# An end of its own for the program behind the last scores: other order on ScalarE, GpSimd and VectorE, and other PSUM banks

## Chip, cores and metric

The kernel runs on one core of one Trainium2 chip. The metric is the device time of one execution in microseconds (us). Engines are written as in the profile: PE is TensorE, PEld its weight loads, ACT ScalarE, DVE VectorE, POOL GpSimd, SP SyncE (it only issues DMAs). Each engine works through its own list of instructions in order and waits for semaphores.

## What is computed

One transformer layer over 16 batches of 256 rows and 128 columns, in float32. Cut to what matters:

```python
x = x + attention(x)            # 16 heads, window of 128, "genetic fitness" weights, exp, values, Wo
x = layernorm(x)
xq = fp4_round(x)               # blocks of 16: scale = max|x| / 6, rounding to the grid 0 .5 1 1.5 2 3 4 6
h = silu(xq @ fp4_round(w_gate).T) * (xq @ fp4_round(w_up).T)      # 352 columns
x = layernorm(x + fp4_round(h) @ fp4_round(w_down).T)
```

## The kernel before

Every batch x goes through some ten stages, and a loop over `t` from -3 works on several batches at once: the scores, exponentials and values of batch t, the projection and first layernorm of batch t - 1, gate and up of the first half of batch t - 2, the second half of batch t - 3, its rounding, the product with w_down ("down") and the second layernorm of batch t - 4. All five engines carry this loop written out, with the same `t`, and the order in each of them is the order of the source. A batch's 256 rows are two halves k = 0 and 1 of 128 rows each. In the 15 iterations or so in the middle PE, DVE and ACT fill each other's gaps.

The last scores belong to batch 15 (B - 1) and are given out at t = 15. What stands behind is the subject here. At t = 16 batch 15 is projected, and from t = 17 to t = 20 nothing is left but the tail: for batches 13, 14 and 15 these steps, each with the engine that does it.

1. `gate_up(x, k)` on PE writes two banks; half 0 goes to WC and WD, half 1 of the last three batches to S bank 0 and 1. `tanh(x, k)` on ACT (line 639, `th`), `gate` and `up` on DVE (lines 1215 and 1222, `hh` and `h`).
2. `h_scale` on DVE (line 1242 to 1250, ends in `hr`), `h_over_scale` on POOL (lines 501 and 505, `hn`), `step_of_h` on ACT (line 616, `hu`), `round_h` on DVE (line 1234 twice for each half, `hm`), `h_times_scale` on POOL (line 511, `hq`).
3. PE turns hq (line 916), for half 0 into WC and for half 1 into WD, at t > 16 into S bank 2. ACT copies it to `hqT` (line 664), and PE multiplies by w_down (line 933) into WD.
4. `residual_2` (line 1202), `sums_2` (line 1169) and `aggr_2` (line 1182) on DVE, `norm_2` on POOL (lines 517 to 522, four small instructions, `rstd` and `nb`), `apply_2` on ACT (line 602, `yo`), and SP stores `yo`.

For the rows of x that go into `gate_up` there is a shorter way: `apply_1` (ACT, `y1`, also line 602), `quant_x` on DVE in seven steps 0 to 6 (line 1259 `xmax` to line 1265 `xn`, then 1269, 1272 and 1276 `xm`), with `step_of_x` on ACT (line 623, `xu`) between step 3 and step 4, then PE turns `xm` (line 966) and ACT copies it to `xaT` (line 706).

Two rules tie batches together. `norm_2(x)` on POOL begins with `need(pool, s_yo, NT * x)`: it waits until ACT has applied batch x - 1, since both use the same small tiles. And `mv2`, `hm`, `hq` and `hqT` exist once, so that each step waits for the readers of the batch before.

Before, the tail is what the loop makes of t = 16 to 20, with conditions such as `if t == B + 1` for the places at which the order should differ. On ACT these are, at the end of t = 16, `apply_1` of batch 15, `apply_2(11)` and `apply_2(12)`, and at t = 17 `tanh(14, 1)`, `step_of_x(15)`, the copies of h^T of batch 13, and so on. On POOL `norm_2(x - 1)` stands between the two halves of `h_times_scale(x)`.

## Time and profile before

| | us |
|---|---|
| median of 3 runs | 336.33 |
| lowest and highest | 336.30, 337.07 |
| profiled execution, its own time | 335.8 |
| span of its trace | 333.8 |
| mean granted TensorE clock, as a share of 2.4 GHz | 0.955 |

| engine | busy us | share of the span |
|---|---|---|
| PE | 264.9 | 79% |
| DVE | 253.2 | 76% |
| ACT | 213.0 | 64% |
| POOL | 198.6 | 59% |

The span is the trace from its first to its last event; 2.0 us of the execution's time lie around it. The busy shares are means over the whole program. In the page's line of 40 slices the digits of PE are 8 and 9 up to slice 35 and then 6, 3, 5, 5, 4, 1: the last 42 us or so are another regime than the middle, and the change lies in them.

### The profile page before, as it was taken

Reading aid. Unit: us, or ns where it says so; the run is one execution under the profiler, and the core shown is the slowest. Engines: PE = TensorE matmul, PEld = TensorE weight load, DVE = VectorE, ACT = ScalarE, POOL = GpSimd, SP = SyncE. Lnnn points to the kernel's source line nnn. Section 1 sums busy time; section 2 is a strip of 40 time slices with the busy share of each in tenths; the row PEclk is TensorE's granted clock in tenths of the full one; section 3 lists DMA queues with packets and bytes.
Section 4 is the critical chain, followed back from the end, with each engine's and each line's share of the span. In section 5 each row is a group of like instructions: output and inputs, shape, how many; then the busy total and the mean of one; then the engine's idle time right before and its main releaser. Section 6 shows DMA issues by size and latency. Waiting matters only on the chain. (4 is left out here: it accounts for less than half of the span.)

```text
span 333.8 us, 12978 instructions
## 1 busy us (share of the span) xinstructions
PE 264.9 (79%) x5044; PEld 177.6 (53%) x5044; DVE 253.2 (76%) x697; ACT 213.0 (64%) x515; POOL 198.6 (59%) x471
## 2 busy tenths in 40 slices
PE   5515778989798998989898989998989999635541
PEld 3313344655466665757575666666656665514330
DVE  5723369476989898989898899999888897836631
ACT  2101535586869787877878787978788896433231
POOL 6363545346485778686869686777873553442541
PEclk9999999999999999999999999999999999975855
DMA  4032112122123313340522233223312100010000
GB/s 120 16 63 50 32 33 49 36 49 51 33 50 35 60 24 84 29 86 20 81 34 65 45 57 40 61 66 34 51 33 60 26 20 18 0 32 2 16 16 21
DMA packets 42884, 14.19 MB, mean 43 GB/s; under 512 B 35586, under 2 KB 42820, under 8 KB 42820
## 3 DMA queue, kind: packets, MB, share of 16 engines
q1 hardware_dynamic: 42820, 13.33, 20.8%
q8 instruction: 41, 0.67, 0.8%
q14 instruction: 23, 0.19, 0.2%
HBM read 2.84 MB, written 2.10 MB: 15 GB/s over the span
## 5 line engine op out<-in xcount | busy, mean ns | idle before, releaser
L596 ACT ACTIVATE Pm<-S 128x384 f32<-128x384 f32 x256 | 112.2, 495 | 51.4 <-PE S L788 51.2
L809 PE MATMUL OT<-Pm,gv 128*32 128x256 f32 (+1 forms) x1024 | 58.3, 348 | 0.0
L782 PE MATMUL S<-BT,AT 32*32 32x160 f16 (+4 forms) x2048 | 41.0, 224 | 16.9 <-ACT Pm L596 10.6
L511 POOL TENSOR_TENSOR hq<-hm,hs 128x352 f32<-128x352 f32 x32 | 24.9, 795 | 36.8 <-DVE hm L1234 36.8
L782 PEld LDWEIGHTS S<-BT,AT 32*32 32x32 f16 x2048 | 17.8, 88 | 50.6 <-ACT Pm L596 34.3
L933 PE MATMUL WD<-wdT,hqT 128*128 128x128 f32 (+1 forms) x192 | 29.0, 307 | 14.7 <-ACT hqT L664 14.7
L809 PEld LDWEIGHTS OT<-Pm,gv 128*32 128x32 f32 x1024 | 27.6, 113 | 20.9 <-issue 8.2
L933 PEld LDWEIGHTS WD<-wdT,hqT 128*128 128x128 f32 (+1 forms) x192 | 25.8, 213 | 17.4 <-ACT hqT L664 17.4
L788 PE MATMUL S<-mask,ident 32*32 32x96 f16 x1024 | 31.3, 207 | 0.0
L853 PE MATMUL WA<-wgv,xT 128*128 128x256 f32 x64 | 22.8, 489 | 4.6 <-DMA bgrow<-bg_dram 3.5
L505 POOL TENSOR_TENSOR hn<-h,hrn 128x352 f32<-128x352 f32 x32 | 25.4, 815 | 1.3
L842 PE MATMUL WC<-wguT,xaT 128*128 128x352 f32 x58 | 24.9, 511 | 0.9 <-ACT xaT L696 0.5
L520 POOL TENSOR_TENSOR rstd<-ve,mhalf 128x2 f32<-128x2 f32 x32 | 23.1, 723 | 0.0
L602 ACT ACTIVATE yo<-y,nb,rstd 128x128 f32<-128x128 f32 x32 | 14.0, 491 | 13.0 <-POOL nb L522 13.0
L843 PE MATMUL WD<-wguT,xaT 128*128 128x352 f32 x58 | 21.9, 459 | 0.0
L557 POOL TENSOR_TENSOR A<-gh,A 128x512 f16<-128x512 f32 x16 | 20.4, 1277 | 0.2
L616 ACT ACTIVATE hu<-hn,off 128x352 f32<-128x352 f32 x32 | 17.6, 615 | 3.4 <-POOL hn L505 3.4
L1215 DVE SCALAR_TENSOR_TENSOR hh<-th,WC 128x352 f32<-128x352 f32 x29 | 14.4, 496 | 5.7 <-ACT th L639 5.4
L1234 DVE SCALAR_TENSOR_TENSOR hm<-hu,hn 128x352 f32<-128x352 f32 x32 | 16.9, 527 | 1.8 <-ACT hu L616 1.8
L683 ACT ACTIVATE gsq<-WA 128x256 f32<-128x256 f32 x16 | 6.2, 386 | 18.7 <-PE WA L857 14.2
L1234 DVE SCALAR_TENSOR_TENSOR hm<-hu,hm 128x352 f32<-128x352 f32 x32 | 17.1, 533 | 0.5
L853 PEld LDWEIGHTS WA<-wgv,xT 128*128 128x128 f32 x64 | 13.3, 231 | 7.7 <-POOL ones L445 3.5
(161 smaller groups left out, 633.6 us busy)
## 6 DMA issues: line engine op xcount, KB each, us to landing
xT<-x_turned_dram SPq DMA_DIRECT2D x16, 128.0 KB, 2.3
...
AT<-A SPq DMA_TRANSPOSE x32, 2.5
BT<-B SPq DMA_TRANSPOSE x32, 2.5
...
```

Source lines behind the costliest of these rows:

```text
L505: pool.tensor_tensor(b3(hn[:, k]), b3(h[:, k]), bc(hrn[:, k], QB), ALU.mult).then_inc(s_hn, 1)
L511: pool.tensor_tensor(b3(hq[:, k, 0:I]), b3(hm[:, k]), bc(hs[:, k], QB), ALU.mult).then_inc(s_hq, 1)
L520: pool.tensor_tensor(r[:, :], ve[:, :], mhalf[:, 0:NT], ALU.pow).then_inc(s_out, 1)
L596: act.activation(Pm[:, group % PR, hd % 4, :], S[:, (H * x + hd) % 3, 0:SCW], ACT.Exp, scale=1.0 / ZS).then_inc(s_exp, 1)
L782: pe.matmul(S[k0:k0 + KG, bank, at:at + n], AT[r:r + 32, x % 2, c, q:q + KG], BT[r:r + 32, x % 2, c, q:q + n], start=(kt == 0), stop=False)
L788: i = pe.matmul(S[k0:k0 + KG, bank, 0:SCW].rearrange("p (b c) -> p b c", c=P)[:, :, k0:k0 + KG], ident16[m:m + KG, m:m + KG], near[m:m + K ...
L809: i = pe.matmul(OT[VP * g:VP * (g + 1), T - (q1 - q0):T], gv_flat[:, at:at + VP], Pm[:, (GROUPS * x + c) % PR, g, q0:q1], start=(kt == 0 a ...
L842: pe.matmul(g, lhs, wguT[:, 0:I], start=True, stop=True).then_inc(s_gate, 1)
L843: pe.matmul(u, lhs, wguT[:, I:2 * I], start=True, stop=True).then_inc(s_gu, 1)
L853: pe.matmul(WA[:, k * 2 * D:(k + 1) * 2 * D], xT[:, (t + 3) % XR, k * P:(k + 1) * P], wgv[:, :], start=(k == 0), stop=False)
L933: i = pe.matmul(WD[:, k * D:(k + 1) * D], hqT[0:kn, k, n * P:(n + 1) * P], wdT[0:kn, n, :], start=(n == 0), stop=(n == 2))
L1234: dve.scalar_tensor_tensor(out=hm[:, k], in0=hu[:, k], scalar=ROUND, in1=hm[:, k] if step else hn[:, k], op0=ALU.max, op1=op).then_inc(s_h ...
```

## The change

The loop over `t` now ends at t = 16 (B) on PE, ACT, DVE and POOL, and the tail is written out behind it on each engine. SP keeps its loop. Same instructions, same number (2153 on PE, 863 on DVE by the program order); what differs is their order and some banks:

- ACT: `tanh(14, 1)` goes ahead of `apply_1` of batch 15, and so ahead of `apply_2(11)` and `apply_2(12)`. The copies of h^T of batch 13 go ahead of these two as well, the `step_of_x` of batch 15 stays behind them. `tanh(15, 1)` goes ahead of `apply_2(13)`, and the last copies of h^T ahead of `apply_2(14)`.
- POOL: both halves of `h_times_scale(x)` go ahead of `norm_2(x - 1)`, for batches 13, 14 and 15.
- DVE: `residual_2`, `sums_2` and `aggr_2` of batch 14 come ahead of the four rounding steps of batch 15, no longer between them.
- PE: the order is the same. The turned hq goes to OT (half 0) and WA (half 1), not to WC and S bank 2, and "down" to S bank 2, not to WD. The waits that go with the banks differ: before, the turned hq of half 0 waited for `h(x + 1, 0)`; now "down" of batch x waits for `residual_2(x - 1)`.

```diff
 # POOL
-            for t in range(FIRST, LAST + 1):
+            for t in range(FIRST, B + 1):
...
-                if live(t - 4) and not late(t - 4):
-                    norm_2(t - 4)
                 if live(t - 3):
                     h_times_scale(t - 3, 1)
+            norm_2(B - 4)
+            for x in (B - 2, B - 1):
+                h_over_scale(x, 0)
+                h_over_scale(x, 1)
+                h_times_scale(x, 0)
+                h_times_scale(x, 1)
+                norm_2(x - 1)
+            norm_2(B - 1)
 # ACT
-                if t == B:
-                    apply_1(t + 1)
-                if live(t - 5) and late(t - 5):
+                if live(t - 5) and t < B:
                     apply_2(t - 5)
-                if live(t - 4) and not late(t - 4):
-                    apply_2(t - 4)
+            def hqT_out(x):
+                for k, bank in enumerate((OT, WA)):
+                    act.wait_ge(s_hqT, NT * x + k + 1)
+                    need(act, s_dn, x)
+                    act.activation(hqT[:, k, :], bank[:, 0:HP], ACT.Copy).then_inc(s_hqTc, 1)
+            tanh(B - 2, 1)
+            apply_1(B + 1)
+            hqT_out(B - 3)
+            apply_2(B - 5)
+            apply_2(B - 4)
+            step_of_x(B - 1)
+            step_of_h(B - 2, 0)
+            step_of_h(B - 2, 1)
+            act.wait_ge(s_xqT, B)
+            act.wait_ge(s_gu, NT * (B - 1))
+            act.activation(xaT[:, T:2 * T], WC[:, T:2 * T], ACT.Copy).then_inc(s_xac, 1)
+            tanh(B - 1, 0)
+            tanh(B - 1, 1)
+            hqT_out(B - 2)
+            apply_2(B - 3)
+            step_of_h(B - 1, 0)
+            step_of_h(B - 1, 1)
+            hqT_out(B - 1)
+            apply_2(B - 2)
+            apply_2(B - 1)
 # PE
+            def hqT_last(x):
+                if x == B - 3:
+                    pe.wait_ge(s_ot, 2 * B)
+                    pe.wait_ge(s_attn, B)
+                else:
+                    pe.wait_ge(s_hqTc, NT * x)
+                for k, bank in enumerate((OT, WA)):
+                    pe.wait_ge(s_hq, NT * x + k + 1)
...
+            def down_last(x):
+                if x > B - 3:
+                    pe.wait_ge(s_ln2, 5 * (x - 1) + 1)
+                for k in range(NT):
+                    pe.wait_ge(s_hqTc, NT * x + k + 1)
+                    for n, (k0, kn) in enumerate(KC):
+                        i = pe.matmul(S[:, 2, k * D:(k + 1) * D], hqT[0:kn, k, n * P:(n + 1) * P], wdT[0:kn, n, :],
...
 # DVE
+            gate(B - 2, 1)
+            up(B - 2, 1)
+            for step in range(3):
+                h_scale(B - 2, step)
+            for step in range(7):
+                quant_x(B - 1, step)
+            down_norm(B - 3)
+            rounds(B - 2)
+            for k in range(NT):
+                gate(B - 1, k)
+                up(B - 1, k)
+            for step in range(3):
+                h_scale(B - 1, step)
+            down_norm(B - 2)
+            rounds(B - 1)
+            down_norm(B - 1)
```

`down_norm(x)` is `residual_2`, `sums_2` and `aggr_2` of x, and `rounds(x)` the four `round_h`.

Three places of the program order, with line numbers of each program's own source. A row is an instruction with what it writes and reads and the semaphores that it waits for.

ACT from the first half's tanh of batch 14 on, before (`y1`, then `yo` of batches 11 and 12, then the second half's tanh):

```order
L639 ACTIVATE th<-WC 128x352 [waits s_hh,s_gate]
L602 ACTIVATE y1<-WB,nb1,rstd1 128x128 [waits s_xq,s_ln2,s_rs1]
L602 ACTIVATE y1<-WB,nb1,rstd1 128x128
L602 ACTIVATE yo<-y2,nb2,rstd2 128x128 [waits st_o1,s_rs2]
L602 ACTIVATE yo<-y2,nb2,rstd2 128x128
L602 ACTIVATE yo<-y2,nb2,rstd2 128x128 [waits st_o0,s_rs2]
L602 ACTIVATE yo<-y2,nb2,rstd2 128x128
L639 ACTIVATE th<-S 128x352 [waits s_hh,s_gate]
L623 ACTIVATE xu<-xn,off 128x256 [waits s_xq]
L664 ACTIVATE hqT<-WC 128x384 [waits s_dn,s_hqT]
L664 ACTIVATE hqT<-S 128x384 [waits s_dn,s_hqT]
```

The same place now:

```order
L642 ACTIVATE th<-WC 128x352 [waits s_hh,s_gate]
L642 ACTIVATE th<-S 128x352 [waits s_hh,s_gate]
L605 ACTIVATE y1<-WB,nb1,rstd1 128x128 [waits s_xq,s_ln2,s_rs1]
L605 ACTIVATE y1<-WB,nb1,rstd1 128x128
L724 ACTIVATE hqT<-OT 128x384 [waits s_dn,s_hqT]
L724 ACTIVATE hqT<-WA 128x384 [waits s_dn,s_hqT]
L605 ACTIVATE yo<-y2,nb2,rstd2 128x128 [waits st_o1,s_rs2]
L605 ACTIVATE yo<-y2,nb2,rstd2 128x128
L605 ACTIVATE yo<-y2,nb2,rstd2 128x128 [waits st_o0,s_rs2]
L605 ACTIVATE yo<-y2,nb2,rstd2 128x128
L626 ACTIVATE xu<-xn,off 128x256 [waits s_xq]
```

The tanh that reads S has moved from behind three pairs of layernorm writes to ahead of them, and the copies of hqT to ahead of `yo`.

POOL from `h_times_scale(13, 0)` to the division of batch 14's h, before (`ve2` to `nb2` is `norm_2`):

```order
L511 TENSOR_TENSOR hq<-hm,hs 128x352 [waits s_hqT,s_hr]
L517 TENSOR_SCALAR ve1<-mv1 128x2 [waits s_ln1]
L518 TENSOR_SCALAR nm1<-mv1 128x2
L520 TENSOR_TENSOR rstd1<-ve1,mhalf 128x2 [waits s_rs1]
L522 TENSOR_TENSOR nb1<-nm1,rstd1 128x2 [waits s_rs1]
L517 TENSOR_SCALAR ve2<-mv2 128x2 [waits s_yo,s_ln2]
L518 TENSOR_SCALAR nm2<-mv2 128x2
L520 TENSOR_TENSOR rstd2<-ve2,mhalf 128x2 [waits s_rs2]
L522 TENSOR_TENSOR nb2<-nm2,rstd2 128x2 [waits s_rs2]
L511 TENSOR_TENSOR hq<-hm,hs 128x352 [waits s_hqT,s_hr]
L501 TENSOR_SCALAR hrn<-hr 128x44 [waits s_hn,s_hs]
```

And now:

```order
L507 TENSOR_TENSOR hq<-hm,hs 128x352 [waits s_hqT,s_hr]
L513 TENSOR_SCALAR ve1<-mv1 128x2 [waits s_ln1]
L514 TENSOR_SCALAR nm1<-mv1 128x2
L516 TENSOR_TENSOR rstd1<-ve1,mhalf 128x2 [waits s_rs1]
L518 TENSOR_TENSOR nb1<-nm1,rstd1 128x2 [waits s_rs1]
L507 TENSOR_TENSOR hq<-hm,hs 128x352 [waits s_hqT,s_hr]
L513 TENSOR_SCALAR ve2<-mv2 128x2 [waits s_yo,s_ln2]
L514 TENSOR_SCALAR nm2<-mv2 128x2
L516 TENSOR_TENSOR rstd2<-ve2,mhalf 128x2 [waits s_rs2]
L518 TENSOR_TENSOR nb2<-nm2,rstd2 128x2 [waits s_rs2]
L497 TENSOR_SCALAR hrn<-hr 128x44 [waits s_hn,s_hs]
```

The second half's hq has moved ahead of `norm_2(12)`.

DVE behind the last `h_scale` (`hr` of batch 15), before (`hm` are the rounding steps):

```order
L1250 RECIPROCAL hr<-hs 128x44 [waits s_hrn,s_hs]
L1234 SCALAR_TENSOR_TENSOR hm<-hu,hn 128x352 [waits s_hq,s_hu]
L1202 TENSOR_TENSOR y2<-y1,WD 128x256 [waits s_yo,s_dn]
L1234 SCALAR_TENSOR_TENSOR hm<-hu,hm 128x352 [waits s_hr]
L1169 BN_STATS st2<-y2 128x6 [waits s_ln2]
L1169 BN_STATS st2<-y2 128x6
L1234 SCALAR_TENSOR_TENSOR hm<-hu,hn 128x352 [waits s_hq,s_hu]
L1182 BN_AGGR mv2<-st2 128x2 [waits s_rs2,s_ln2]
L1182 BN_AGGR mv2<-st2 128x2
L1234 SCALAR_TENSOR_TENSOR hm<-hu,hm 128x352 [waits s_hr]
```

And now:

```order
L1316 RECIPROCAL hr<-hs 128x44 [waits s_hrn,s_hs]
L1268 TENSOR_TENSOR y2<-y1,S 128x256 [waits s_yo,s_dn]
L1234 BN_STATS st2<-y2 128x6 [waits s_ln2]
L1234 BN_STATS st2<-y2 128x6
L1247 BN_AGGR mv2<-st2 128x2 [waits s_rs2,s_ln2]
L1247 BN_AGGR mv2<-st2 128x2
L1300 SCALAR_TENSOR_TENSOR hm<-hu,hn 128x352 [waits s_hq,s_hu]
L1300 SCALAR_TENSOR_TENSOR hm<-hu,hm 128x352 [waits s_hr]
L1300 SCALAR_TENSOR_TENSOR hm<-hu,hn 128x352 [waits s_hq,s_hu]
L1300 SCALAR_TENSOR_TENSOR hm<-hu,hm 128x352 [waits s_hr]
```

The five instructions of batch 14's residual and layernorm have moved ahead of batch 15's four rounding steps.

## Rows read from the trace of the kernel before

**Rows 1.** Waits from 290 to 334 us: total us, times, longest us

```profile
ACT yo L602 <- POOL nb L522: 13.0, 4, 4.9
...
DVE y L1202 <- PE WD L933: 7.5, 2, 5.6
```

**Rows 2.** Timeline, ACT: start us, us, engine, line, operation, out<-in, count, [idle before <-releaser]

```profile
293.72 0.81 ACT L602 ACTIVATE y<-WB,nb,rstd 128x128 f32<-128x128 f32 x2 [1.67 <-POOL nb L522]
...
294.42 0.87 ACT L602 ACTIVATE yo<-y,nb,rstd 128x128 f32<-128x128 f32 x2
...
297.70 0.44 ACT L639 ACTIVATE th<-S 128x352 f32<-128x352 f32 x1
...
302.79 0.51 ACT L623 ACTIVATE xu<-xn,off 128x256 f32<-128x256 f32 x1 [4.65 <-DVE xn L1265]
...
303.20 0.47 ACT L664 ACTIVATE hqT<-WC 128x384 f32<-128x384 f32 x1
```

**Rows 3.** Timeline, POOL and then ACT, around `norm_2(12)`

```profile
295.48 0.19 POOL L517 TENSOR_SCALAR ve<-mv 128x2 f32<-128x2 f32 x1 [1.79 <-ACT yo L602]
...
296.84 0.79 POOL L511 TENSOR_TENSOR hq<-hm,hs 128x352 f32<-128x352 f32 x1
...
296.91 0.88 ACT L602 ACTIVATE yo<-y,nb,rstd 128x128 f32<-128x128 f32 x2 [1.62 <-POOL nb L522]
```

**Rows 4.** Timeline, DVE, batches 14, 15 and 13 in the tail

```profile
298.17 0.52 DVE L1215 SCALAR_TENSOR_TENSOR hh<-th,S 128x352 f32<-128x352 f32 x1 [4.49 <-ACT th L639]
...
302.10 0.65 DVE L1265 SCALAR_TENSOR_TENSOR xn<-y,xr 128x256 f32<-128x256 f32 x1
...
304.32 0.43 DVE L1276 TENSOR_TENSOR xm<-xg,xs 128x256 f32<-128x256 f32 x1
...
306.69 0.42 DVE L1202 TENSOR_TENSOR y<-y,WD 128x256 f32<-128x256 f32 x1 [1.95 <-PE WD L933]
...
307.89 0.49 DVE L1234 SCALAR_TENSOR_TENSOR hm<-hu,hn 128x352 f32<-128x352 f32 x1
...
312.95 0.52 DVE L1215 SCALAR_TENSOR_TENSOR hh<-th,S 128x352 f32<-128x352 f32 x1 [1.57 <-ACT th L639]
```

**Rows 5.** Timeline, PE, "down" at either clock and the gate products

```profile
285.21 1.60 PE L933 MATMUL WD<-wdT,hqT 128*128 128x128 f32 x12 [0.72 <-ACT hqT L664]
...
290.69 0.86 PE L842 MATMUL WC<-wguT,xaT 128*128 128x352 f32 x2 [0.47 <-ACT xaT L696]
...
291.98 0.76 PE L842 MATMUL S<-wguT,xaT 128*128 128x352 f32 x2
...
303.73 2.93 PE L933 MATMUL WD<-wdT,hqT 128*128 128x128 f32 x12 [5.15 <-ACT hqT L664]
...
306.45 0.63 PE L966 MATMUL WC<-identf,xm 128*128 128x128 f32 x2
...
307.56 0.86 PE L842 MATMUL WC<-wguT,xaT 128*128 128x352 f32 x2 [0.47 <-ACT xaT L706]
```

**Rows 6.** Windows of 1 us: busy us of PE, PEld, DVE, ACT, POOL, then PEclk, DMA, GB/s

```profile
296.00:297.00 1.00, 0.00 (x0) 0.00 (x0) 0.00 (x0) 0.09 (x1) 0.92 (x3) 0.94 0.44 131
...
307.00:308.00 1.00, 0.53 (x3) 0.34 (x3) 0.88 (x6) 0.39 (x1) 0.00 (x0) 0.94 0.00 0
```

**Rows 7.** Timeline, all engines, batch 15 from its first rounding step to its end

```profile
317.54 0.53 DVE L1234 SCALAR_TENSOR_TENSOR hm<-hu,hn 128x352 f32<-128x352 f32 x1 [1.84 <-ACT hu L616]
...
318.91 0.79 POOL L511 TENSOR_TENSOR hq<-hm,hs 128x352 f32<-128x352 f32 x1 [1.28 <-DVE hm L1234]
...
319.14 0.94 DVE L1234 SCALAR_TENSOR_TENSOR hm<-hu,hn 128x352 f32<-128x352 f32 x1
...
321.86 0.79 POOL L511 TENSOR_TENSOR hq<-hm,hs 128x352 f32<-128x352 f32 x1
...
326.21 0.42 DVE L1202 TENSOR_TENSOR y<-y,WD 128x256 f32<-128x256 f32 x1 [5.57 <-PE WD L933]
...
329.07 0.88 ACT L602 ACTIVATE yo<-y,nb,rstd 128x128 f32<-128x128 f32 x2 [4.94 <-POOL nb L522]
```

More of the change, by code:

```diff
@@ L639, in tanh @@
                 act.activation(th[:, k, :], gate_up_at(x, k)[0], ACT.Tanh, scale=0.5).then_inc(s_th, 1)
-            for t in range(FIRST, LAST + 1):
+            for t in range(FIRST, B + 1):
                 if t > 0:
@@ L655, in _ @@
                 exps(t, 2)
-                if live(t - 2) and t != B + 1:
+                if live(t - 2):
                     apply_1(t)
@@ L660, in _ @@
                 if live(t - 4):
-                    for k, bank in enumerate((WC, WD if t <= B else S[:, 2])):
+                    for k, bank in enumerate((WC, WD)):
                         act.wait_ge(s_hqT, NT * (t - 4) + k + 1)
@@ L889, in fitness_sums @@
                 pe.matmul(WA[:, 0:H], onesf[:, :], rden[:, H:2 * H], start=False, stop=True).then_inc(s_sum, 1)
-            for t in range(FIRST, LAST + 1):
+            for t in range(FIRST, B + 1):
                 if t > 0:
@@ L912, in _ @@
                     after_last(pe, (t - 3, s_h, h_done(t - 3)))
-                    for k, bank in enumerate((WC, WD if t <= B else S[:, 2])):
+                    for k, bank in enumerate((WC, WD)):
                         pe.wait_ge(s_hq, NT * (t - 4) + k + 1)
@@ L984, in _ @@
                 values(t, 2)
+            def hqT_last(x):
[6 more added lines that the diff above has]
+                    pe.wait_ge(s_hq, NT * x + k + 1)
+                    for n in range(3):
+                        i = pe.transpose(bank[:, n * P:(n + 1) * P], hq[:, k, n * P:(n + 1) * P], identf[:, :])
+                    i.then_inc(s_hqT, 1)
+            def down_last(x):
[5 more added lines that the diff above has]
+                        i = pe.matmul(S[:, 2, k * D:(k + 1) * D], hqT[0:kn, k, n * P:(n + 1) * P], wdT[0:kn, n, :],
+                                      start=(n == 0), stop=(n == 2))
+                i.then_inc(s_dn, 1)
+            pe.wait_ge(s_h, NT * (B - 3) + 2)
+            gate_up(B - 2, 1, *gate_up_at(B - 2, 1))
+            hqT_last(B - 3)
+            down_last(B - 3)
+            pe.wait_ge(s_h, NT * (B - 2) + 1)
+            pe.wait_ge(s_xq, 7 * B)
+            for k in range(NT):
+                i = pe.transpose(WC[:, T + k * P:T + (k + 1) * P], xm[:, k * D:(k + 1) * D], identf[:, :])
+            i.then_inc(s_xqT, 1)
+            pe.wait_ge(s_xac, B + 2)
+            gate_up(B - 1, 0, *gate_up_at(B - 1, 0))
+            pe.wait_ge(s_h, NT * (B - 2) + 2)
+            gate_up(B - 1, 1, *gate_up_at(B - 1, 1))
+            hqT_last(B - 2)
+            down_last(B - 2)
+            hqT_last(B - 1)
+            down_last(B - 1)
             pe.wait_ge(s_okmin, 3)
@@ L1277, in quant_x @@
                 i.then_inc(s_xq, 1)
-            for t in range(FIRST, LAST + 1):
+            for t in range(FIRST, B + 1):
                 if live(t + 1):
@@ L1336, in _ @@
                     h_scale(t - 3, 2)
-                if t == B + 1:
-                    for step in range(7):
-                        quant_x(t - 2, step)
-                    residual_2(t)
-                    sums_2(t - 4)
-                    aggr_2(t - 4)
                 if live(t - 2) and t < B:
@@ L1379, in _ @@
                     round_h(t - 3, 0, 0)
-                if live(t - 4) and t != B + 1:
-                    residual_2(t)
+                if live(t - 4):
+                    residual_2(t - 4)
                 if live(t - 3):
                     round_h(t - 3, 0, 1)
-                if live(t - 4) and t != B + 1 and not late(t - 4):
+                if live(t - 4) and not late(t - 4):
                     sums_2(t - 4)
@@ L1390, in _ @@
                     round_h(t - 3, 1, 0)
-                if live(t - 4) and t != B + 1 and not late(t - 4):
+                if live(t - 4) and not late(t - 4):
                     aggr_2(t - 4)
@@ L1428, in _, with down_norm, rounds @@
                     sizes_in_range()
+            def down_norm(x):
+                residual_2(x)
+                sums_2(x)
+                aggr_2(x)
+            def rounds(x):
+                for k in range(NT):
+                    round_h(x, k, 0)
+                    round_h(x, k, 1)
+            gate(B - 2, 1)
[6 more added lines that the diff above has]
+            rounds(B - 2)
+            for k in range(NT):
+                gate(B - 1, k)
[5 more added lines that the diff above has]
+            down_norm(B - 1)
             dve.wait_ge(s_oksum, 1)
```

33 lines of the change are left out of this document (14 added, 19 removed).

## Prediction

> **What bounds the kernel now.** I read the 40 slices first: PE is busy 8 to 9 tenths until slice 35, then 6 tenths and less, so the last 42 us are no longer bound by an engine but by a chain between engines. The waits of that stretch name the links [rows 1]: ACT waits for `nb` of the second layernorm (13.0 us in 4 waits) and DVE for "down" (7.5 us in 2). The timeline of each engine then shows where a ready instruction stands behind one that waits. There are three such places.
>
> First, ACT. The four products of `gate_up` in a row begin at 290.69, the S half, `gate_up(14, 1)`, is written from 291.98 on, its first bank by 292.74 [rows 5], but its tanh begins at 297.70 [rows 2], since the `yo` of batches 11 and 12 stand ahead of it, and the second of these waits for POOL [rows 3]. DVE was free at 293.68 and waited 4.49 us for that tanh [rows 4]. Second, PE: the turning of batch 15's `xm` at 306.45 follows a "down" that began only at 303.73 [rows 5], because the copy of h^T on ACT stood behind the `xu` of 302.79 [rows 2]. `xm` itself was ready at 304.75 [rows 4]. Third, the end: `hq(15, 1)` stands behind `norm_2(14)` on POOL and begins at 321.86, while its last rounding step ended near 320.65 (one more step of 0.53 behind the one from 319.14 to 320.08, and a gap) [rows 7]. The time of the execution is the span plus 2.0 us, and the span ends 3.8 us or so after the last `yo`, with its store.
>
> **The sum, step by step.** I follow the chain with the same durations and the same distances between dependent steps as before.
>
> Step 1, tanh(14, 1) ahead of `yo`. It is ready at about 292.8, lasts 0.44, and DVE is busy until 293.68. So gate(14, 1) begins at 293.7 and not at 298.17: 4.5 us earlier. Its cover is DVE's own work, and nothing is late.
>
> Step 2, `xu(15)`. From gate(14, 1) to `xn` is 3.93 us before (302.10 - 298.17), so `xn` ends at 298.3 [rows 4]. ACT is the late one now. `y1` ends at 294.5 [rows 2]; the two h^T copies of batch 13 take 0.47 each and the second waits for hq(13, 1). That is ready at 294.5 and no more at 297.6, since POOL does it right behind rstd(15) and not behind `norm_2(12)` [rows 3]; turned by PE, its copy ends at 295.6. `yo(11)` follows, 0.87 us, until 296.4. Then the round trip: before, `yo(11)` ended at 295.29 and `yo(12)` began at 296.91, 1.62 us, all of it POOL's `norm_2(12)` [rows 3]. So `yo(12)` runs from 298.05 to 298.95, and `xu(15)` begins at 298.9 and not at 302.79: 3.9 us earlier. The change leaves 0.6 us here. What waits behind `yo(12)` is `xu`, both `hu` of batch 14 and through them DVE and POOL.
>
> Step 3, PE's turn. From `xu` to the end of `xm` is 1.96 us (304.75 - 302.79), so `xm` is ready at 300.85 [rows 2, 4]. The "down" of batch 13 begins now at about 295.2 and lasts 1.60 to 2.93 us [rows 5], so it is over by 298.2 and holds nobody. PE turns `xm` at 300.9, against 306.45: 5.5 us earlier. `residual_2(13)` on DVE comes directly behind `xm`, at 300.9 against 306.69, 5.8 us earlier, and with it the rounding of batch 14: 302.1 against 307.89 [rows 4].
>
> Step 4, gate(15, 1). DVE did gate(15, 0) and up(15, 0) before and was idle for 1.57 us when gate(15, 1) began at 312.95; it was thus free at 311.38, now 5.8 us earlier, at 305.6. The tanh no longer stands behind `yo(13)`. It needs the third of four products. These start 1.1 us behind the turning (307.56 - 306.45), so at 302.0, and the third is written 2.05 us later at the full clock, at 304.05 (291.98 + 0.76 - 290.69). For the low clock I estimate 1.83 times that, from the 12 "down" products that took 2.93 us at low and 1.60 at full clock [rows 5]: 305.75, and gate(15, 1) at 306.2, which is 0.6 late. Which clock it is is not seen in the trace of before. There the share falls to 0.94 in 296 to 297 after an idle PE, and comes back in 307 to 308, after PE had worked without a pause from 303.73 on [rows 5, 6]. PE is idle from 297 to 300.9 now, so the products start low; I take the middle, 0.3 us late, and gate(15, 1) at 305.9 against 312.95: 7.05 us earlier.
>
> Step 5, `residual_2(14)` ahead of the rounding. From gate(15, 1) to the first rounding step are 4.59 us (317.54 - 312.95), of which DVE was idle for 1.84, waiting for `hu` [rows 7]. The five moved instructions take 1.2 us, by the same five of batch 13 (307.89 - 306.69) [rows 4], and fit in there if "down" of batch 14 is over by 309.2. hq(14, 1) is ready at about 305.4, PE turns it, ACT copies it, "down" takes 1.6 to 2.9: between 308.3 and 309.6. This is a new wait, with between 0 and 0.6 us to pay; I take 0.3. Rounding begins at 310.8 against 317.54.
>
> Step 6, the last rounding and hq(15, 1). Before, these took 317.54 to 320.65 with batch 14's residual in between. Now the four steps stand together, 0.53 each; one will be stretched to 0.94 beside POOL's hq(15, 0), as at 319.14 beside 318.91 [rows 7]. That makes 2.5 us, and with 0.05 hq(15, 1) begins at 313.35 against 321.86: 8.5 us earlier. `norm_2(14)` goes behind it and is hidden by PE's "down", 4.35 us from hq(15, 1) to `residual_2(15)` [rows 7].
>
> Step 7, from hq(15, 1) to the last `yo` nothing changes; the trace of before has it at the low clock throughout. The other banks cost nothing: OT and WA have no reader left in the tail, and the wait of "down" for the residual of the batch before is met in every case by a microsecond or more.
>
> The sum is -8.5 us. Against the profiled execution 335.8 - 8.5 = 327.3. The median is 0.5 above that execution, so 336.33 - 8.5 = **327.8 us**.
>
> The Trainium skill, "GPSIMD Engine Reference", section Key points, says that GpSimd shares its SBUF interfaces with VectorE, so that DVE instructions with two SBUF inputs contend. By that rule the first `xg` step of batch 15, which now falls beside the two `hn` of batch 14, would be stretched as well. The sum would be 0.4 us less, 328.2; the one stretched rounding of the rows agrees with the rule.
>
> **Rivals.**
>
> (a) *The low clock stays.* In this form the four products and all PE work behind them run low. "Down" of batch 14 then ends near 311.6 (products until 306.9; two turnings of some 0.9 each, by 0.63 for two blocks at 306.45 [rows 5] and three here; a copy of 0.47 [rows 2]; 2.93 us), and since `residual_2(14)` now stands ahead of the rounding on DVE, rounding starts at 313.3 and not 310.8: 2.5 us back, 330.3 us. For it: PE is idle for 4 us ahead of the products, longer than before, where "down" ran directly into them. Against it: the products are a burst of some 3 to 4 us themselves. The Trainium skill, "TensorE: Matmul & The Clock Gate", section "Why this matters for your kernels", asks for short idle gaps between bursts, which speaks for (a).
>
> (b) *The clock is up at the end.* Before, the last turnings and "down" took 4.35 us at the low clock. At full they would take about 2.85 (1.33 us less for the 12 products [rows 5], and by estimate 0.2 for the turning ahead of them), and with the 0.3 of step 4 the time is 326.0. For it: PE's last burst is 9 us earlier. Against it: there is still an idle gap of 3 to 4 us ahead of it, and the gap of 294 to 297 was followed by the low clock [rows 6].
>
> (c) *ACT becomes the bound, and slower.* ACT stands at `yo(12)` until POOL has done `norm_2(12)`, which waits for `yo(11)` on ACT itself. `yo(11)` was pushed back by two copies and the tanh. Each us by which this round trip is late moves `xu(15)` and everything. It decides from a trip of 1.62 + 8.5 = 10.1 us; then the kernel is as slow as before, at 12 it is 338.2. Against it: 1.62 us were measured with the same neighbours, and POOL has only hq(13, 1), 0.79 us, ahead.
>
> (d) *It does only the last part.* If the x path is not freed (`xm` still turned at 306), only step 6 is left, 1.2 us for the order on POOL and 0.8 for gate(15, 1): 334.3 us. Against it: the order listings show all three moves.
>
> **How the numbers follow.** Forecast 0.72 (327.0 to 329.0), (a) 0.12, (b) 0.07, (d) 0.04, (c) 0.02, and 0.03 for a gain so small that it can't be told. The range goes from (b) to (a), 326.0 to 330.3. About 0.3%, 1 us, is what a measurement of this kernel can tell from no change: faster 0.95, same 0.03, slower 0.02.
>
> **What would show it.** gate(14, 1) on DVE directly behind h(14, 0) at 293.7; `xu(15)` at 298.9 directly behind `yo(12)`; `xm` turned at 300.9; gate(15, 1) at 305.9; rounding of batch 15 from 310.8; hq(15, 1) at 313.4 with `norm_2(14)` behind it; last `yo` at 320.5, span 325.3. Step 4 is wrong if the granted share is 1.00 or 0.50 throughout 302 to 307, step 5 if DVE waits for "down" of batch 14 longer than 0.6 us. The whole is wrong if ACT idles more than 2 us ahead of `yo(12)`, or if t = 3 to 16 take another time than before.

## The result, and the profile after

| | before | after |
|---|---|---|
| median us, 4 runs each | 336.70 | 328.64 |
| lowest and highest | 336.30, 339.24 | 327.95, 329.88 |
| ratio with 95% interval | | 0.974 (0.969 to 0.979) |
| profiled execution, own time | 335.8 | 328.11 |
| span of its trace | 333.8 | 326.3 |
| from the copy to `xaT` of batch 14 to the end of the last `yo` | 39.70 | 32.43 |

The change takes 8.1 us off the median (2.1 to 3.1%), and 7.5 us off the span. The last line of the table is the tail by itself: it begins where ACT starts the copy to `xaT` of batch 14 (290.25 us before, 289.90 after) and leaves out what the loop ahead of it does. Nearly all of the gain lies in it, 7.3 us in this execution; the loop ahead was 0.35 us shorter.

The waits of the stretch from 290 us on, in total, times, longest; they answer to [rows 1]:

```profile
ACT yo L605 <- POOL nb L518: 5.6, 2, 4.0
...
DVE y L1268 <- PE S L1029: 4.7, 2, 4.4
```

ACT's wait for `nb` has gone from 13.0 us in 4 to 5.6 us in 2, DVE's for "down" from 7.5 to 4.7, of which 4.4 is the very last one.

The timeline of ACT (start, duration), the lines that answer to [rows 2, 3]:

```profile
293.89 0.46 ACT L642 ACTIVATE th<-S 128x352 f32<-128x352 f32 x1 [1.51 <-PE S L867]
...
294.94 0.50 ACT L724 ACTIVATE hqT<-OT 128x384 f32<-128x384 f32 x1
...
295.68 0.90 ACT L605 ACTIVATE yo<-y,nb,rstd 128x128 f32<-128x128 f32 x2
...
298.20 0.88 ACT L605 ACTIVATE yo<-y,nb,rstd 128x128 f32<-128x128 f32 x2 [1.62 <-POOL nb L518]
...
298.98 0.49 ACT L626 ACTIVATE xu<-xn,off 128x256 f32<-128x256 f32 x1
```

The S half's tanh stands first now, the copies next, then `yo` of batches 11 and 12 with the round trip through POOL between them (1.62 us, as before), and `xu` directly behind.

DVE's lines for [rows 4]: gate(14, 1), the first `xg`, gate(15, 1), and `residual_2(14)`.

```profile
294.39 0.52 DVE L1281 SCALAR_TENSOR_TENSOR hh<-th,S 128x352 f32<-128x352 f32 x1 [0.72 <-ACT th L642]
...
299.57 0.84 DVE L1335 SCALAR_TENSOR_TENSOR xg<-xu,xn 128x256 f32<-128x256 f32 x1 [0.83 <-ACT xu L626]
...
307.04 0.52 DVE L1281 SCALAR_TENSOR_TENSOR hh<-th,S 128x352 f32<-128x352 f32 x1 [1.09 <-ACT th L642]
...
310.02 0.42 DVE L1268 TENSOR_TENSOR y<-y,S 128x256 f32<-128x256 f32 x1 [0.23 <-PE S L1029]
```

PE's for [rows 5]: the turning of `xm`, the first gate product of batch 15, "down" of batches 14 and 15.

```profile
301.48 0.66 PE L1040 MATMUL WC<-identf,xm 128*128 128x128 f32 x2 [4.38 <-DVE xm L1342]
...
302.61 1.54 PE L867 MATMUL WC<-wguT,xaT 128*128 128x352 f32 x2 [0.47 <-ACT xaT L736]
...
308.40 1.58 PE L1029 MATMUL S<-wdT,hqT 128*128 128x128 f32 x12 [0.34 <-ACT hqT L724]
...
315.78 2.77 PE L1029 MATMUL S<-wdT,hqT 128*128 128x128 f32 x12
```

The granted clock, in windows of 1 us with the columns of [rows 6]:

```profile
289.00:290.00 1.00, 0.86 (x7) 0.61 (x7) 1.00 (x4) 0.10 (x1) 0.00 (x0) 0.97 0.00 0
...
293.00:294.00 1.00, 1.00 (x5) 0.57 (x4) 0.52 (x1) 0.11 (x1) 0.92 (x3) 0.83 0.00 0
...
300.00:301.00 1.00, 0.00 (x0) 0.00 (x0) 0.93 (x3) 0.60 (x2) 0.13 (x1) 0.59 0.44 131
...
307.00:308.00 1.00, 1.00 (x8) 0.66 (x6) 0.93 (x2) 0.23 (x2) 0.23 (x2) 1.00 0.00 0
...
313.00:314.00 1.00, 0.07 (x1) 0.10 (x2) 0.97 (x2) 0.00 (x0) 0.79 (x1) 0.91 0.00 0
```

Worked out from the shares, it was low from about 289.9 to 293.3 (the products of batch 14), from 300.2 to 307.0 (those of batch 15) and from 313.8 on. And the end, for [rows 7]:

```profile
311.62 0.53 DVE L1300 SCALAR_TENSOR_TENSOR hm<-hu,hn 128x352 f32<-128x352 f32 x1 [0.33 <-ACT hu L619]
...
312.79 1.00 POOL L507 TENSOR_TENSOR hq<-hm,hs 128x352 f32<-128x352 f32 x1 [1.07 <-DVE hm L1300]
...
313.18 0.99 DVE L1300 SCALAR_TENSOR_TENSOR hm<-hu,hm 128x352 f32<-128x352 f32 x1
...
314.25 0.79 POOL L507 TENSOR_TENSOR hq<-hm,hs 128x352 f32<-128x352 f32 x1 [0.46 <-DVE hm L1300]
...
318.58 0.42 DVE L1268 TENSOR_TENSOR y<-y,S 128x256 f32<-128x256 f32 x1 [4.42 <-PE S L1029]
...
321.45 0.88 ACT L605 ACTIVATE yo<-y,nb,rstd 128x128 f32<-128x128 f32 x2 [4.02 <-POOL nb L518]
```

### The profile page after: what moved, and what is told of

Read it like the earlier page. It is cut to its first block and busy times, and to the rows that moved or that the text cites. A ratio compares the mean times of both kernels' runs of the same rounds, so it can differ in the third digit from the quotient of the medians.

```text
span 326.3 us, 12978 instructions
## 1 busy us (share of the span) xinstructions
PE 265.4 (81%) x5044; PEld 177.6 (54%) x5044; DVE 255.0 (78%) x697; ACT 213.0 (65%) x515; POOL 196.6 (60%) x471
## 5 line engine op out<-in xcount | busy, mean ns | idle before, releaser
L956 PE MATMUL WD<-wdT,hqT 128*128 128x128 f32 x156 | 20.9, 283 | 8.9 <-ACT hqT L665 8.9
L867 PE MATMUL WC<-wguT,xaT 128*128 128x352 f32 x58 | 26.3, 536 | 0.9 <-ACT xaT L697 0.5
L956 PEld LDWEIGHTS WD<-wdT,hqT 128*128 128x128 f32 x156 | 18.4, 191 | 10.9 <-ACT hqT L665 10.9
L868 PE MATMUL WD<-wguT,xaT 128*128 128x352 f32 x58 | 23.1, 482 | 0.0
L612 ACT ACTIVATE OTs<-OT 128x256 f32<-128x256 f32 x32 | 12.4, 387 | 7.3 <-PE OT L834 7.3
```

The costliest lines, as they stand in the source:

```text
L867: pe.matmul(g, lhs, wguT[:, 0:I], start=True, stop=True).then_inc(s_gate, 1)
L868: pe.matmul(u, lhs, wguT[:, I:2 * I], start=True, stop=True).then_inc(s_gu, 1)
L956: i = pe.matmul(WD[:, k * D:(k + 1) * D], hqT[0:kn, k, n * P:(n + 1) * P], wdT[0:kn, n, :], start=(n == 0), stop=(n == 2))
```

## Experiments

The theories. **A**: the gain is what the order gives, above all on ACT, and the clock shifts it by a microsecond or so. **B**: a clock that happened to be up (first form) or the other banks (second form) carry a good part. Some runs have rivals of their own. Where a difference is small I compare the tail as defined above, or its length up to hq(15, 1) on POOL, the last multiplication before the last "down", since whole executions of one kernel differ by up to 4 us through the loop ahead of the tail (last section).

| kernel | median us | ratio to before (95%) | tail us | tail to hq(15, 1) |
|---|---|---|---|---|
| before | 336.70 | | 39.70 | 31.61 |
| after, first trace | 328.64 | 0.974 (0.969 to 0.979) | 32.43 | 24.35 |
| after, again | 327.68 | 0.976 (0.968 to 0.985) | 31.80 | 23.72 |
| tanh undone in after | 333.13 | 0.992 (0.987 to 0.997) | 36.51 | 28.59 |
| tanh alone in before | 333.12 | 0.989 (0.983 to 0.995) | 36.57 | 28.67 |
| POOL alone in before | 337.88 | 1.006 (1.002 to 1.010) | 41.85 | 31.54 |
| DVE undone in after | 329.81 | 0.981 (0.975 to 0.987) | 32.39 | 24.30 |
| POOL undone in after | 328.85 | 0.977 (0.971 to 0.984) | 32.94 | 24.86 |
| banks undone in after | 328.67 | 0.976 (0.969 to 0.983) | 31.99 | 24.42 |
| PE kept busy | 327.61 | 0.977 (0.968 to 0.986) | 29.61 | 22.93 |
| round trip moved | 330.24 | 0.978 (0.973 to 0.983) | 32.58 | 24.50 |
| copies undone in after | 329.03 | 0.976 (0.973 to 0.980) | 32.63 | 24.55 |
| round trip moved and PE kept busy | 325.65 | 0.966 (0.963 to 0.968) | 28.73 | 22.05 |

### The changed kernel again

> The changed kernel once more, beside the kernel before on the same chip, as the ground for the other three. Theory A (the gain is the sum of the moves in the order, and the granted clock only shifts it by a microsecond): 328 to 330 us, 7 to 9 below the kernel before; gate(15, 1) begins right behind its tanh, and if the four gate products of batch 15 run at the full clock this time, it begins about 1.1 us earlier than the 307.0 of the first trace, measured from gate(14, 1). Theory B (a good part of the gain is the clock, which happened to be up for the down products of batches 13 and 14): where these run low, the gain falls below 5 us.

Measured 327.68 us, a little below the range that I had given. DVE's lines for gate(14, 1) and gate(15, 1):

```profile
293.82 0.52 DVE L1281 SCALAR_TENSOR_TENSOR hh<-th,S 128x352 f32<-128x352 f32 x1
...
306.80 0.52 DVE L1281 SCALAR_TENSOR_TENSOR hh<-th,S 128x352 f32<-128x352 f32 x1 [1.09 <-ACT th L642]
```

In this trace the clock was up through the products of batch 14 and gate(14, 1) came 1.0 us earlier in the tail than in the first trace (3.53 us behind the copy to `xaT`, against 4.49). From there on the two traces are alike, the low clock in the products of batch 15 included. So the clock at one place is worth 0.6 us of the tail (31.80 against 32.43). "Down" of batches 13 and 14 ran at the full clock in both, so that this run alone does not try B in its first form; the run with the copies undone does.

### The tanh, undone and alone

```diff
-            tanh(B - 2, 1)
             apply_1(B + 1)
             hqT_out(B - 3)
             apply_2(B - 5)
             apply_2(B - 4)
+            tanh(B - 2, 1)
             step_of_x(B - 1)
```

> One move undone in the changed kernel: tanh(14, 1) again behind the second-layernorm writes of batches 11 and 12, everything else as changed. Theory A: gate(14, 1) waits until about 299.2 instead of 294.4, and all that follows, but for what the x path gives back, is 4 to 4.5 us later: 332.5 us. Theory B (the banks or the clock carry the gain, and the x path, which waits for the same ACT writes anyway, hides the tanh): under 1 us, 329 to 330.

Measured 333.13 us. The timeline of DVE and ACT:

```profile
300.00 0.52 DVE L1281 SCALAR_TENSOR_TENSOR hh<-th,S 128x352 f32<-128x352 f32 x1 [5.50 <-ACT th L642]
...
304.62 0.51 ACT L626 ACTIVATE xu<-xn,off 128x256 f32<-128x256 f32 x1 [4.64 <-DVE xn L1331]
```

gate(14, 1) is back at 8.9 us behind the copy to `xaT`, where the repeated run has 3.5, `xu` is 5.1 us later, and the tail is 4.7 us longer. Of the 5.4 us at gate(14, 1) the x path gives back 0.7: 0.3 at `xu`, which no longer waits for `yo(12)`, and 0.4 at `xg`, which takes 0.43 us here. The rest arrives at the end. The same move done by itself in the kernel before:

```diff
+                if t == B:
+                    tanh(B - 2, 1)
                     apply_1(t + 1)
...
-                if live(t - 3):
+                if live(t - 3) and t != B + 1:
                     tanh(t - 3, 1)
```

> One move alone, done in the kernel before: tanh(14, 1) ahead of the first-layernorm write of batch 15, nothing else. Theory A: gate(14, 1) at 293.7 instead of 298.2, so 4.5 us less from there on, 331.5 to 332.5 us. The sum of this and of the loss in the kernel with that move undone need not be the whole. Theory B (without the other banks PE still waits for the readers of WC and holds the chain): under 2 us gain, 334.5 to 336.

Measured 333.12 us, 3.1 us off the tail and not 4.5. DVE, ACT and PE show where the rest went:

```profile
298.48 0.19 DVE L1247 TENSOR_SCALAR hs<-hmax 128x44 f32<-128x44 f32 x1 [1.49 <-POOL hq L511]
...
300.63 0.51 ACT L623 ACTIVATE xu<-xn,off 128x256 f32<-128x256 f32 x1 [2.08 <-DVE xn L1266]
...
301.57 2.93 PE L934 MATMUL WD<-wdT,hqT 128*128 128x128 f32 x12 [2.59 <-ACT hqT L664]
...
304.29 0.64 PE L967 MATMUL WC<-identf,xm 128*128 128x128 f32 x2
```

gate(14, 1) is 4.4 us earlier in the tail (3.54 against 7.92 us), but the second step of `h_scale` of batch 14 then waits 1.49 us for hq(13, 1), since both use `hs`, and hq(13, 1) still stands behind `norm_2(12)` on POOL. So `xu` is only 2.9 us earlier (9.61 against 12.54), and so are the turning of `xm`, gate(15, 1) and hq(15, 1); the other 0.2 us of the 3.1 are a last "down" of 2.59 us, before 2.77. "Down" of batch 13, at the low clock behind the late copies of h^T, does hold `xm`, which was ready at 302.6, by 1.7 us. This is the second place of my prediction, but it is no loss against the kernel before, where `xm` was held just as long (304.75 to 306.45). In the changed kernel hq(13, 1) is ahead of `norm_2(12)` and DVE does not wait there, so the full gain of the tanh rests on that move of POOL's; no run undoes it by itself. By tail length the tanh is 3.1 us of 7.3 to 7.9 alone and 4.7 as the last one in.

### POOL, alone and undone

```diff
-                if live(t - 4) and not late(t - 4):
-                    norm_2(t - 4)
                 if live(t - 3):
                     h_times_scale(t - 3, 1)
+                if live(t - 4) and not late(t - 4):
+                    norm_2(t - 4)
```

> One move alone, done in the kernel before: on POOL both halves of h_times_scale(x) ahead of norm_2(x - 1), in the tail only. Theory A says that this move is worth nothing by itself and costs: norm_2(13) is now behind hq(14, 1), so that the write yo(13) on ACT is about 1 to 1.6 us later, and tanh(15, 1), which stands behind it there, too; hq(15, 1) gains back what it stood behind norm_2(14). In all +0.5 to +2.4 us, 337 to 338.5. Rival C, by the third part of my prediction (the end gains 1.2 us from this order): 335 us.

Measured 337.88 us, 0.2 to 1.0% slower than before, by the tail 2.15 us. POOL, ACT and PE at the end:

```profile
321.20 0.79 POOL L511 TENSOR_TENSOR hq<-hm,hs 128x352 f32<-128x352 f32 x1 [1.03 <-DVE hm L1234]
...
323.50 0.88 ACT L602 ACTIVATE yo<-y,nb,rstd 128x128 f32<-128x128 f32 x2 [4.77 <-POOL nb L522]
...
324.80 2.93 PE L933 MATMUL WD<-wdT,hqT 128*128 128x128 f32 x12 [1.86 <-ACT hqT L664]
```

Both halves of the theory are there: `yo(13)` comes 1.1 us later in the tail (22.5 against 21.4), tanh and gate(15, 1) with it, and hq(15, 1) wins that 1.1 back (31.54 against 31.61). The loss is behind that, and I had not seen it: `norm_2(14)` now follows hq(15, 1), `yo(14)` on ACT waits for it until 323.50, and the copies of h^T of batch 15 stand behind `yo(14)` there. "Down" begins 3.6 us behind hq(15, 1), before 1.5. Rival C fell. Undone in the changed kernel, for the last two batches only (hq(13, 1) stays ahead of `norm_2(12)`):

```diff
                 h_times_scale(x, 0)
-                h_times_scale(x, 1)
                 norm_2(x - 1)
+                h_times_scale(x, 1)
```

> One move undone in the changed kernel: on POOL norm_2(x - 1) of the last two batches again between the halves of h_times_scale(x). Theory A, by the first trace: norm_2(13) takes its 1.45 us between hq(14, 0) and hq(14, 1), which delays the down of batch 14 by at most 0.5 us behind the gate products, and norm_2(14) pushes hq(15, 1) from 314.0 to about 315.3, since hq(15, 0) ends at 313.6: 1 to 1.4 us later in all, 329 us. Rival E (POOL's order is free either way, as the kernel before with this move alone was 1.6 us slower): no change.

Measured 328.85 us. POOL:

```profile
312.44 1.00 POOL L507 TENSOR_TENSOR hq<-hm,hs 128x352 f32<-128x352 f32 x1 [1.07 <-DVE hm L1300]
...
315.03 0.79 POOL L507 TENSOR_TENSOR hq<-hm,hs 128x352 f32<-128x352 f32 x1
```

hq(15, 1) is pushed from 23.72 to 24.86 us, the tail is 1.14 longer than in the repeated run, at the same clock states. The medians, 328.85 and 327.68, differ in the same way, but their intervals overlap; the tail is the evidence. So this order on POOL costs 2.2 us in the old program and, for two of its three batches, gains 1.1 in the new. As the traces show it, what decides is whether the last copies of h^T stand behind `yo(14)` on ACT; no run moves these copies alone.

### DVE undone

```diff
+            round_h(B - 1, 0, 0)
+            residual_2(B - 2)
+            round_h(B - 1, 0, 1)
+            sums_2(B - 2)
+            round_h(B - 1, 1, 0)
+            aggr_2(B - 2)
+            round_h(B - 1, 1, 1)
-            down_norm(B - 2)
-            rounds(B - 1)
             down_norm(B - 1)
```

> One move undone in the changed kernel: on DVE the residual, sums and means of batch 14 again between the four rounding steps of batch 15. Theory A: in the changed kernel the 1.2 us of these instructions lie in DVE's wait for hu(15, 0), which is otherwise 1.8 us long. Undone, they come back into the chain: from the first rounding step to hq(15, 1) it takes 3.5 to 3.7 us instead of 2.6, the end is 0.9 to 1.1 us later, about 329 us. Rival D (the new wait for the down product of batch 14 takes back what the move gains): under 0.3 us.

Measured 329.81 us, the tail 0.6 us longer than in the repeated run:

```profile
311.13 0.53 DVE L1300 SCALAR_TENSOR_TENSOR hm<-hu,hn 128x352 f32<-128x352 f32 x1 [1.84 <-ACT hu L619]
...
311.57 0.41 DVE L1268 TENSOR_TENSOR y<-y,S 128x256 f32<-128x256 f32 x1
...
312.73 0.93 DVE L1300 SCALAR_TENSOR_TENSOR hm<-hu,hn 128x352 f32<-128x352 f32 x1
...
313.74 0.48 DVE L1300 SCALAR_TENSOR_TENSOR hm<-hu,hm 128x352 f32<-128x352 f32 x1
...
314.31 0.79 POOL L507 TENSOR_TENSOR hq<-hm,hs 128x352 f32<-128x352 f32 x1 [1.02 <-DVE hm L1300]
```

From the first rounding step to hq(15, 1) it takes 3.18 us, and 2.63 in the changed kernel. The direction is A's, the size 0.55 and not 1. One rounding step is stretched beside hq(15, 0) in either (0.99 and 0.93). The insertions cost less than the 1.12 us that they are busy, since instructions in a row overlap on DVE: the residual starts at 311.57, before the rounding step ahead of it ends at 311.66. The last rounding step ends 3.09 us behind the start of the first, in the changed kernel 2.55. Rival D, under 0.3 us, is out.

### The banks undone

```diff
-                for k, bank in enumerate((OT, WA)):
+                if x < B - 1:
+                    pe.wait_ge(s_h, NT * (x + 1) + 1)
+                for k, bank in enumerate((WC, S[:, 2])):
...
-                        i = pe.matmul(S[:, 2, k * D:(k + 1) * D], hqT[0:kn, k, n * P:(n + 1) * P], wdT[0:kn, n, :],
+                        i = pe.matmul(WD[:, k * D:(k + 1) * D], hqT[0:kn, k, n * P:(n + 1) * P], wdT[0:kn, n, :],
```

> The banks undone in the changed kernel, the order kept: turned hq to WC and S bank 2, down to WD, with the waits for the readers of these banks. Theory A, as in my prediction (the other banks cost nothing and gain nothing by themselves): the turning of batch 13 has to wait for h(14, 0), which is done when the gate products end, and that of batch 14 for h(15, 0) at 305.9, which is before these end at 307.2. The same time as the changed kernel, 327.5 to 328.5 us. Theory B (the banks carry part of the gain): over 1 us more.

Measured 328.67 us. PE, the last gate product and the turning of batch 14:

```profile
307.26 1.15 PE L868 MATMUL S<-wguT,xaT 128*128 128x352 f32 x2
...
308.25 0.49 PE L1021 MATMUL WC<-identf,hq 128*128 128x128 f32 x3
```

The turning follows the product without a pause, though it now also waits for h(15, 0). Up to hq(15, 1) this tail is 24.42 us, the changed kernel's with the same clock in batch 14 is 24.35. B's second form is out: the banks are worth nothing here, with the waits for their readers in place. (The rest of this tail is 0.5 us shorter because the clock came back in the last "down", 2.24 us.)

### PE kept busy

```diff
             down_last(B - 3)
+            pe.wait_ge(s_y1, NT * B)
+            fill(5)         # 5 x matmul(WB[:, 0:I], identf, wguT[:, 0:I])
             pe.wait_ge(s_h, NT * (B - 2) + 1)
...
             down_last(B - 2)
+            fill(5)
             hqT_last(B - 1)
```

> The changed kernel with ten products added that nobody reads (identity by the gate and up weights, 352 columns, into the free bank WB), five behind the down of batch 13 and five behind that of batch 14, where PE is idle for 4 us: does the granted clock stay up, and what is it worth? Theory A: the clock stays at full in the gate products of batch 15, the third of them is written 2.05 us behind the first instead of 3.9, gate(15, 1) on DVE directly follows up(15, 0), 1.05 us earlier; and the last turning and down take 2.85 us instead of 4.35: 325.3 us, 2.5 less than the changed kernel. If only the first happens, 326.7. If the added products run at the low clock they end after xm is ready and cost up to 3 us.

The ten products go into a bank that nobody reads. The profiled execution took 325.68 us, 2.2 less than that of the repeated run (327.91), and the tails say the same, 29.61 against 31.80. The median, 327.61, carries two executions of 329.5 and 330.6 and can't be told from the 327.68 of the repeated run; the tails are the evidence, and the last run below. DVE and PE:

```profile
305.76 0.52 DVE L1289 SCALAR_TENSOR_TENSOR hh<-th,S 128x352 f32<-128x352 f32 x1 [0.21 <-ACT th L642]
...
314.27 1.68 PE L1034 MATMUL S<-wdT,hqT 128*128 128x128 f32 x12
```

The clock fell in the middle of the first gate product (0.83 in 302 to 303, 0.50 in 303 to 304), after PE had been idle from 299.4 to 301.1, but gate(15, 1) came 15.64 us into the tail and not 16.51. Behind the second filling the clock stayed: the last "down" took 1.68 us and not 2.77, and from hq(15, 1) to `residual_2(15)` it is 2.94 us against 4.34. The clock is thus worth 2.2 us of the 31.8, bought with products that are thrown away: 0.9 up to gate(15, 1) and 1.4 behind hq(15, 1), less 0.1 in between.

### The round trip

```diff
 # POOL: norm_2(B - 4) behind the two h_over_scale(B - 2, k)
 # ACT
-            apply_2(B - 4)
             step_of_x(B - 1)
             step_of_h(B - 2, 0)
             step_of_h(B - 2, 1)
+            apply_2(B - 4)
```

> The changed kernel with its round trip taken out of the way of batch 15's x: on POOL norm_2(12) behind the two divisions of batch 14's h, on ACT apply_2(12) behind step_of_x(15) and step_of_h(14). Theory F (POOL's hn beside DVE's xg is what stretches xg from 0.43 to 0.84 us in the changed kernel, in every trace of it): hn now starts 0.6 us earlier and ends before or shortly after xg begins, xg takes 0.43 to 0.6, xu(15) begins 0.04 us behind xn, together 0.4 to 0.6 us less, about 327.3. Rival G (xg is stretched by something else, for instance by its own place, or what is won before the gate products is lost at the later yo(12), which now stands ahead of the copy to xaT): xg stays at 0.84, the time within 0.2 us of the changed kernel.

Measured 330.24 us, with an execution of 332.39 profiled whose loop was 3.7 us late; its tail is 32.58, and 32.43 is that of the first trace, which had the same clock in batch 14.

```profile
301.87 1.71 POOL L501 TENSOR_TENSOR hn<-h,hrn 128x352 f32<-128x352 f32 x2
...
302.28 0.65 DVE L1332 SCALAR_TENSOR_TENSOR xn<-y,xr 128x256 f32<-128x256 f32 x1
...
303.58 0.43 DVE L1336 SCALAR_TENSOR_TENSOR xg<-xu,xn 128x256 f32<-128x256 f32 x1 [0.64 <-ACT xu L627]
...
305.49 0.88 ACT L606 ACTIVATE yo<-y,nb,rstd 128x128 f32<-128x128 f32 x2 [1.05 <-POOL nb L518]
```

F is right on the stretching: with `hn` moved away, `xg` takes 0.43 us. But `hn` now lies beside `xn`, which takes 0.65 and not 0.43. The turning of `xm` is 0.3 us earlier in the tail (11.27 against 11.58). Then the second half of rival G takes over: `yo(12)` at 305.49 stands ahead of the copy to `xaT`, and the gate products begin 12.87 us into the tail, in the first trace 12.71. In sum the tail gains nothing.

### The copies undone

```diff
             apply_1(B + 1)
-            hqT_out(B - 3)
             apply_2(B - 5)
             apply_2(B - 4)
             step_of_x(B - 1)
+            hqT_out(B - 3)
             step_of_h(B - 2, 0)
```

> Another move undone in the changed kernel: the copies of h^T of batch 13 on ACT again behind step_of_x(15), as before the change. Theory A now says that this move gained nothing: PE has 4 us to spare ahead of xm, while the two copies push yo(11), and so norm_2(12), yo(12) and hn, back by 0.9 us. Undone, yo(12) ends about 0.9 us earlier, xu(15) begins when xn is done, 0.3 to 0.5 us earlier, hn falls ahead of xg, which returns to 0.43 us, and down of batch 13 ends at about 300.7, just ahead of the turning of xm: 0.3 to 0.8 us less, about 327.2. Rival H (PE has no room for this down, and the turning of xm waits for it, as in the kernel before): 0.5 us or more later, over 328.4.

Measured 329.03 us, the tail 0.8 us longer than in the repeated run. H holds:

```profile
298.85 0.51 ACT L626 ACTIVATE xu<-xn,off 128x256 f32<-128x256 f32 x1 [0.62 <-DVE xn L1331]
...
299.46 0.43 DVE L1335 SCALAR_TENSOR_TENSOR xg<-xu,xn 128x256 f32<-128x256 f32 x1 [0.64 <-ACT xu L626]
...
299.79 2.93 PE L1029 MATMUL S<-wdT,hqT 128*128 128x128 f32 x12 [4.31 <-ACT hqT L724]
...
302.51 0.63 PE L1040 MATMUL WC<-identf,xm 128*128 128x128 f32 x2
```

`xu` and `xg` are as A said (`xu` 8.15 us into the tail against 8.46, `xg` at 0.43). But PE was idle until 299.79, the clock had fallen at 297.4, and "down" took 2.93 us instead of 1.60 and held `xm`, ready at 300.81, until 302.5. I had counted with the full clock. At the full clock it would have ended 1.3 us earlier, by estimate (2.93 - 1.60), and held `xm` by 0.4 us. The early copies thus pay by having PE do this "down" before the clock falls, and not by their own 0.9 us.

This run also tries B in its first form: with "down" of batch 13 at the low clock the tail is still 7.1 us shorter than before (32.63 against 39.70). "Down" of batch 14 ran at the full clock in every variant of the changed kernel, so that its part in (a) of the prediction was not tried.

### Both

> Both together, to see whether they add: the round trip out of the way and PE kept busy, now with seven unread products behind the down of batch 13 and five behind that of batch 14. With five, the clock fell in the middle of the first gate product and gate(15, 1) still waited 0.7 us for its tanh. Theory A: gate products at the full clock, gate(15, 1) directly behind up(15, 0), the last turning and down in 2.9 us, and 0.5 us from the x path: profile at 324.7 to 325.2 us, the median 3 us below the changed kernel. Rival: the clock falls all the same at the first pause, since 1.5 us of idle PE remain ahead of xm; then 325.2 to 325.7.

Measured 325.65 us, ratio 0.966 (0.963 to 0.968); the best kernel of this study. I had expected 324.7 to 325.2; the time lies where the rival had it, though the fall of the clock on which the rival rested did not occur. The profiled execution is one whose loop was slow (328.5), the other four took 325.4 to 325.9.

```profile
305.52 0.86 PE L868 MATMUL WC<-wguT,xaT 128*128 128x352 f32 x2 [1.18 <-ACT xaT L737]
...
308.49 0.52 DVE L1290 SCALAR_TENSOR_TENSOR hh<-th,S 128x352 f32<-128x352 f32 x1
```

gate(15, 1) follows gate(15, 0) and up with no wait at all, the clock stayed at 1.00 from 286 to beyond the last `yo`. Of the tail's 28.73 us there are 3.1 us less than in the repeated run. The tail is 0.9 us shorter than with the five products alone, and the rows divide that. The gate products begin at the same place in both (11.87 and 11.86 us into the tail), but run at the full clock here, so that gate(15, 1) loses its wait of 0.2 us for the tanh. The rest is DVE: it was done with up(15, 0) 15.4 us into the tail there and 14.8 here, since `residual_2(13)` came 0.7 us earlier. So the moved round trip does bring about 0.6 us where the products are not the late ones; no run has the seven products without it.

## Why the prediction was right, point by point

Forecast 327.8 us, 8.5 less; measured 328.64, 8.1 less by medians and 7.3 or 7.9 by the tails of two traces. The chain that I followed is the one in the traces, and the miss of 0.6 to 1.2 us by tail has its place in steps 3 and 4. The moves undone one at a time cost 4.7 (tanh), 1.1 (POOL, two batches), 0.8 (copies of batch 13), 0.6 (DVE) and 0 us (banks): 7.2 of the 7.9. Not tried by themselves are hq(13, 1) ahead of `norm_2(12)`, `tanh(15, 1)` ahead of `yo(13)` and the last copies of h^T ahead of `yo(14)`.

**Step 1** (4.5 us). The mechanism holds, by the move undone (4.7 us longer) and alone (gate(14, 1) 4.4 us earlier, of which 3.1 reach the end). In the first trace gate(14, 1) came at 294.39 and not at 293.7, because the products of batch 14, which I took at the full clock as before, ran low there. In the repeated one it was 293.82.

**Step 2** (`xu` at 298.9). 298.98 and 298.75. The round trip of 1.62 us was found to the hundredth, `yo(12)` began at 298.20 (298.05 forecast). I took the 3.93 us from gate(14, 1) to `xn` as given; it holds only because POOL has hq(13, 1) done early, as the lone tanh showed, and the sum did not say so.

**Step 3** (turning at 300.9). 301.48 and 301.25. This term was mis-sized: I took the 1.96 us from `xu` to the end of `xm` from a place where `hn` was over. Here `xg` lies beside `hn` and takes 0.84 us instead of 0.43, in both traces and in the four variants with the same order up to there (DVE, POOL and banks undone, PE kept busy). This is what the Trainium skill, "GPSIMD Engine Reference", section Key points, says of DVE instructions with two SBUF inputs, and the 0.4 us that I set beside the sum for it were real.

**Step 4** (gate(15, 1) at 305.9). 307.04 and 306.80. The sign and the mechanism held; the tanh was the late one, by 1.09 us. I had put the clock in the middle, and it was low for all three products that matter: the third was written 3.89 us behind the start of the first (302.61 to 306.50), where I had estimated 3.75 for the low clock. By the sign that I had set (a share of 0.50 throughout 302 to 307) this step is wrong in its clock: there was no middle. So my term was too good by 0.6 us by place of the turning and 0.5 by the clock. The Trainium skill, "TensorE: Matmul & The Clock Gate", section "Why this matters for your kernels", asks for short idle gaps between bursts, and the trace agrees: PE idle from 297.1, clock down at 300.2. But in the same trace the clock had also fallen at 289.9, behind a gap of only 1.7 us.

**Step 5** (0.3 us lost to "down" of batch 14; its latest end of 309.6 gives that, and not the 0.6 that I named as the bound). Nothing lost: `residual_2(14)` began at 310.02, 0.23 us late, and still DVE waited another 0.33 for `hu`. "Down" took 1.58 us, as the clock was back at 307.0.

**Step 6** (hq(15, 1) at 313.35). 314.25 and 314.01. From the first rounding step to it are 2.63 us, forecast 2.55, with the one stretched step as told. **Step 7**: from hq(15, 1) to the end of the last `yo` 8.08 us, before 8.09.

**The rivals.** (a) came half: the gate products ran low, but the clock returned before "down" of batch 14, so that it cost 0.5 us and not 2.5. Its working has a slip: the terms as I listed them give 312.1 for the end of "down" and not 311.6, and the 313.3 and 2.5 us follow from 312.1. The "12 products" of "down" are six, with two rows each in the trace; the ratio of 1.83 stays, but the gate products, at 1.17 us each against 0.59, went by 2.0. (b) did not occur by itself in any trace of the changed kernel, and with PE kept busy it did, at 2.2 us. (c) did not occur; the trip stayed at 1.62 us. (d) did not; with the copies undone its mechanism is there ("down" of batch 13 behind `xu` holds the turning by 1.7 us), and costs 0.8 us. The sizes that I gave in (d), 1.2 us for POOL and 0.8 for gate(15, 1), can't be added up by themselves: POOL's order alone cost 2.2 us.
